# An SSM layer with a butterfly FFN on one core: another order of the work of its first two phases, and its step values brought to tokens by transposes

## What is computed

```
xn       = layernorm(x)
xi, z    = split(xn @ in_proj.T)               # 512 and 512 features
xc       = silu(conv of 4 taps over time(xi) + conv_b)
d, B, C  = xc @ x_proj.T                       # 1 + 16 + 16 values per token
delta    = softplus(d)
h        = h * exp(-delta * exp(A_log)) + xc * delta * B     # the scan, state of 512 x 16
y        = (h @ C + xc * D) * silu(z)
x        = x + y @ out_proj.T
h        = butterfly_up(layernorm(x) @ W_exp + b_exp)        # 1024 features, 10 stages of 2 x 2 mixings
x        = x + butterfly_down(gelu(h + up_bias)) @ W_con + b_con + down_bias
```

## Time and profile before

| | us |
| --- | --- |
| median of 3 runs | 568.64 (566.94 to 570.74) |
| the profiled execution | 569.59, its span 567.9 |
| TensorE busy | 528.9 (93% of the span), weight loads 430.3 (76%) |
| VectorE busy | 409.6 (72%) |
| ScalarE busy | 306.1 (54%) |
| GpSimd busy | 109.5 (19%) |
| mean granted clock of TensorE | 0.966 |

### The profile page before, as it was taken

How to read it: one execution, slowest core, us unless ns; L and a number is a source line. 1 busy time by engine, 2 the same in 40 slices (tenths; PEclk the granted TensorE clock), 3 DMA queues, 4 the chain that set the end, 5 groups by cost and what they waited for, 6 DMA issues and landing times.

```text
span 567.9 us, 8152 instructions
## 1 busy us (share of the span) xinstructions
PE 528.9 (93%) x2996; PEld 430.3 (76%) x2996; DVE 409.6 (72%) x860; ACT 306.1 (54%) x526; POOL 109.5 (19%) x96
## 2 busy tenths in 40 slices
PE   3998899888999999999999999999999999699896
PEld 3766676776897779887888778877888788578886
DVE  4859999587983799468966799379946894575532
ACT  2876883865239622874268623962287417431342
POOL 4042100230201301050103120130105021411110
PEclk9986979799999999999999999999999999799999
DMA  8542311200012001210112001200021002100011
GB/s 244 97 27 3 80 35 38 76 2 2 23 52 74 4 2 48 66 39 2 37 41 74 0 9 68 71 8 1 5 73 38 0 2 74 41 1 0 6 34 37
DMA packets 42619, 21.75 MB, mean 38 GB/s; under 512 B 26419, under 2 KB 41011, under 8 KB 42580
## 3 DMA queue, kind: packets, MB, share of 16 engines
q1 hardware_dynamic: 39940, 17.57, 13.0%
q10 hardware_dynamic: 2640, 3.67, 2.3%
HBM read 16.78 MB, written 4.46 MB: 37 GB/s over the span
## 4 chain that ended last, share of the span: by engine, by line
PE 48%; DVE 20%; issue 12%; ACT 9%; SPq 6%; POOL 3%; DMA 0%; DVEq 0%; ACTq 0%; POOLq 0%
PE wide L711 12%; PE acc L844 9%; PE wide L833 7%; SPq L420 5%; PE wide L822 4%; DVE xc L1552 2%; DVE xc L1555 2%; POOL x1b_xn L598 2%; DVE state L1516 2%; DVE hid_low L1429 2%; PE wide L804 2%; PE small L731 2%; PE wide L811 2%; DVE xc L1412 2%; ACT L1054 2%
## 5 line engine op out<-in xcount | busy, mean ns | idle before, releaser
L1054 ACT ACTIVATE hid_f<-wide,bias_up 128x512 f32<-128x512 f32 x64 | 44.0, 687 | 162.0 <-PE wide L833 161.6
L1412 DVE SCALAR_TENSOR_TENSOR xc<-xi,taps,xc 128x512 f32<-128x512 f32 x96 | 87.0, 911 | 4.0 <-ACT xc L1085 1.7
L844 PE MATMUL acc<-w_down_high,hid_high 128*128 128x256 f32 x256 | 73.2, 286 | 5.6 <-DVE hid_low L1429 5.4
L844 PE MATMUL acc<-w_down_high,hid_low 128*128 128x256 f32 x256 | 71.9, 281 | 0.0
L844 PE MATMUL acc<-w_down_low,hid_high 128*128 128x256 f32 x256 | 71.9, 281 | 0.0
L1429 DVE TENSOR_TENSOR hid_low<-hid_f,hid_high 128x512 fp32r<-128x512 f32 x64 | 46.3, 725 | 29.8 <-ACT hid_high L1163 29.2
L833 PE MATMUL wide<-xnT_ln2T_high,w_up_high 128*128 128x512 f32 x128 | 55.4, 432 | 3.4 <-DVE xnT_ln2T_low L1423 1.8
L522 POOL TENSOR_TENSOR rstd<-var_eps,minus_half 128x4 f32<-128x4 f32 x16 | 19.1, 1192 | 202.8 <-DVE var_eps L1317 202.8
L711 PE MATMUL wide<-xnT_ln1T_high,w_in_high 128*128 128x512 f32 x128 | 56.5, 441 | 1.1 <-DVE xnT_ln1T_low L1423 1.0
L822 PE MATMUL wide<-w_out,xc 128*128 128x256 f32 x256 | 56.7, 379 | 0.3 <-DVE xc L1555 0.3
L844 PEld LDWEIGHTS acc<-w_down_high,hid_high 128*128 128x128 f32 x256 | 48.0, 188 | 11.2 <-issue 8.2
(11 more groups left out here) (185 smaller groups left out, 1054.6 us busy)
## 6 DMA issues: line engine op xcount, KB each, us to landing
x_res<-in_L_attn_x_dram SPq DMA_DIRECT2D x9, 512.0 KB, 3.5
c_near<-c_of_tokens SPq DMA_DIRECT2D x8, 512.0 KB
out_dram<-x1b_xn SPq DMA_DIRECT2D x8, 512.0 KB, 2.9
x_ln<-in_L_attn_x_dram SPq DMA_DIRECT2D x7, 512.0 KB, 3.6
xc<-in_L_attn_in_proj_w_dram ACTq DMA_DIRECT2D x2, 512.0 KB, 7.1
xc<-in_L_ffn_W_exp_dram ACTq DMA_DIRECT2D x1, 1024.0 KB, 10.8
x1b_xn<-in_L_ffn_W_con_dram ACTq DMA_DIRECT2D x1, 1024.0 KB, 14.5
raw_out<-n_L_attn_out_proj_w_dram ACTq DMA_DIRECT2D x1, 512.0 KB, 7.0
```

What stands on the lines that cost most here:

```text
L844: last = pe.matmul(acc[:, c, :], hid[h][:, j % HRING, c * P:(c + 1) * P], w_down[w][:, j, 0:DM], start=j == 0 and c % 2 == 0 and n == 0, s ...
L1054: ins = act.activation(out_ap, in_ap, how.pop("func"), **how)
L1412: ins = dve.scalar_tensor_tensor(xc[u % BATCH][:, e, :], xi[:, e, tap:tap + TILE], taps[:, e, tap:tap + 1], xc[u % BATCH][:, e, :], ALU.mu ...
```

## The change

Three things are changed, in phases 0 and 1 but for the first.

- `xd_tokens_first` transposes the blocks of `xdT` against the identity, 128 x 128 each, in place of multiplying them by `fold`; VectorE adds the two halves as it takes them, with a `tensor_reduce` in place of the copy. `fold` and its semaphore go.
- In phase 0, B comes ahead of the second unit's first input projection; the C products and the state inputs follow after four projections, and the steps of the weights are placed anew. On VectorE the convolutions are spread over the phase, and the diagonal comes behind them; `advance_state` comes ahead of `assemble`, and the third DOWN mixing, the short and whole DOWN paths and the third unit's normalisation come behind the gates. On ScalarE the first DOWN scaling comes behind the first two taps, the silu of z 0 and of x 1 ahead of later copies, and only the first UP scaling is left in phase 0. VectorE waits for the zeroed tiles later.
- In phase 1, VectorE does all three UP mixings, ScalarE the second and third scalings, the weights' steps come later, and w_down is made in two steps (17 and 18).

```diff
         w_x = sb("w_x", [P, CB, HALF])
-        fold = sb("fold", [P, XD])
         w_out = sb("w_out", [P, CB, DM])
...
         rates_exp = sem("rates_exp")
-        folded = sem("folded")
         made = sem("made")
...
 [("w_up", 1, 0), ("w_up", 1, 1)],
-[("w_down", q, 0) for q in range(4)],
+[("w_down", q, 0) for q in range(2)],
+[("w_down", q, 0) for q in range(2, 4)],
         ]
...
     for c in range(GR):
-        last = pe.matmul(bank[:, c * P:c * P + XD], xdT[:, c * P:(c + 1) * P], fold[:, :], start=True, stop=True)
+        last = pe.transpose(bank[:, c * P:(c + 1) * P], xdT[:, c * P:(c + 1) * P], ident[:, :])
     mark_written(last, "xdtok", 0, u)
...
     tokens_first(0)
-    pe.wait_ge(folded, 1)
     xd_tokens_first(0)
+    transposes(1, "ln1T", x_ln, norm1)
     prepare(4)
     prepare(5)
-    prepare(6)
-    transposes(1, "ln1T", x_ln, norm1)
     pe.wait_ge(masks_made, 2)
...
     step_sums(0)
+    decayed_b(0)
     in_projection(1, 0)
-    prepare(7)
     in_projection(1, 1)
-    decayed_b(0)
-    prepare(8)
+    prepare(6)
     in_projection(1, 2)
-    decayed_c_start(0)
-    prepare(9)
+    prepare(7)
     in_projection(1, 3)
+    decayed_c_start(0)
     decayed_c_block(0)
-    prepare(10)
-    in_projection(1, 4)
     state_inputs(0)
-    prepare(11)
+    prepare(8)
+    in_projection(1, 4)
+    prepare(9)
     in_projection(1, 5)
-    prepare(12)
-    in_projection(1, 6)
     off_diagonal(0)
+    prepare(10)
+    in_projection(1, 6)
+    prepare(11)
     in_projection(1, 7)
+    prepare(12)
     prepare(13)
     ssm_output(0)
-    prepare(14)
-    transposes(2, "ln1T", x_ln, norm1)
     wait_all_taken("w_out")
     out_projection(0, 0)
+    transposes(2, "ln1T", x_ln, norm1)
+    prepare(14)
     out_projection(0, 1)
...
     in_or_none(v, 5)
-    beside("in 5")
     decayed_c_start(u)
     in_or_none(v, 6)
-    beside("in 6")
     decayed_c_block(u)
     state_inputs(u)
+    beside("state inputs")
     in_or_none(v, 7)
+    beside("in 7")
     off_diagonal(u)
...
     up(p, 2)
+    beside("up 2")
     down(p, 0)
...
 def weights_of_ffn(place):
-    if place == "in 5":
+    if place == "state inputs":
         prepare(15)
-    elif place == "in 6":
+    elif place == "in 7":
         prepare(16)
     elif place == "products":
+        prepare(17)
         wait_all_taken("w_up")
     elif place == "up 1":
-        prepare(17)
+        prepare(18)
+    elif place == "up 2":
         wait_all_taken("w_down")
...
     exp_abs(0)
+    high_parts(1, "ln1T")
     prepare(4)
     prepare(5)
-    scale_blocks(DOWN, 0)
     place_halo(1)
-    high_parts(1, "ln1T")
     exp_sums(0)
-    scale_blocks(DOWN, 1)
+    exp_gaps(0)
     first_tap(1, 0)
-    scale_blocks(DOWN, 2)
     first_tap(1, 1)
-    exp_gaps(0)
-    prepare(8)
-    first_tap(1, 2)
-    take_c_start(0)
+    scale_blocks(DOWN, 0)
     exp_diagonal(0)
-    prepare(9)
+    first_tap(1, 2)
     first_tap(1, 3)
     save_halo(1)
+    take_c_start(0)
     take_c_block(0)
-    prepare(10)
-    copy_z(1, 4)
     copy_first_state(0)
-    prepare(11)
+    scale_blocks(DOWN, 1)
+    prepare(8)
+    copy_z(1, 4)
+    prepare(9)
     copy_z(1, 5)
-    prepare(12)
-    copy_z(1, 6)
-    copy_z(1, 7)
     silu_z(0)
+    prepare(10)
+    copy_z(1, 6)
+    prepare(11)
     silu_x(1)
+    copy_z(1, 7)
+    prepare(12)
+    scale_blocks(DOWN, 2)
     silu_z(1)
     scale_blocks(UP, 0)
-    scale_blocks(UP, 1)
     high_parts(2, "ln1T")
...
     exp_sums(u)
+    beside("sums")
     if v < UNITS:
...
         copy_z(v, 5)
+    beside("gaps")
     take_c_start(u)
     exp_diagonal(u)
-    beside("diagonal")
     if v < UNITS:
...
         copy_z(v, 7)
+    beside("z 7")
     copy_first_state(u)
+    beside("first state")
     gelu(p, 0)
...
 def weights_of_ffn(place):
-    if place == "abs":
+    if place == "sums":
+        scale_blocks(UP, 1)
+    elif place == "gaps":
         scale_blocks(UP, 2)
-    elif place == "diagonal":
-        prepare(15)
     elif place == "z 6":
+        prepare(15)
+    elif place == "z 7":
         prepare(16)
-    elif place == "gelu 1":
+    elif place == "first state":
         prepare(17)
+    elif place == "gelu 1":
+        prepare(18)

...
     dve.wait_ge(rates_exp, 1)
-    dve.tensor_tensor(fold[:, :], ident[:, 0:XD], ident[:, HALF:HALF + XD], ALU.add).then_inc(folded, 1)
     dve.tensor_reduce(row_in_block[:, :], ident[:, :].rearrange("p (j u) -> p u j", u=BL), AXIS_X, ALU.add)
...
                            rates[:, :].unsqueeze(1).to_broadcast([P, NB, NS]), ALU.mult))
-    dve.wait_ge(zeroed, 2)

...
     written(dve, u, "xdtok", 0)
-    mark_read(dve.tensor_copy(xd[:, :, :], tile_of("xdtok", 0, u)[:, :]
-                              .rearrange("p (c w) -> p c w", w=P)[:, :, 0:XD]), "xdtok", 0, u)
+    mark_read(dve.tensor_reduce(xd[:, :, :], tile_of("xdtok", 0, u)[:, :]
+                                .rearrange("p (c h w) -> p c w h", h=2, w=HALF)[:, :, 0:XD, :], AXIS_X, ALU.add), "xdtok", 0, u)
     read(dve, u, "xdtok", 0)
...
     take_xd(0)
+    dve.wait_ge(zeroed, 2)
     softplus(0)
-    multiply_short_paths(UP)
-    sum_biases()
     low_parts(1, "ln1T")
     take_sums(0)
-    add_blocks(DOWN, 0)
-    add_blocks(DOWN, 1)
-    multiply_whole_paths(UP)
+    sum_biases()
     weigh(0)
-    add_blocks(DOWN, 2)
     weigh_b(0)
-    for e in range(CB):
-        convolve(1, e)
+    convolve(1, 0)
+    multiply_short_paths(UP)
+    add_blocks(DOWN, 0)
+    convolve(1, 1)
+    multiply_whole_paths(UP)
+    convolve(1, 2)
+    convolve(1, 3)
+    add_blocks(DOWN, 1)
     diagonal_times_c(0)
     sum_diagonal(0)
-    assemble(0)
     advance_state(0)
-    multiply_short_paths(DOWN)
+    assemble(0)
     first_stats(2)
...
     gate(0, 1)
-    first_normalise(2)
     gate(0, 2)
     gate(0, 3)
+    first_normalise(2)
+    multiply_short_paths(DOWN)
+    add_blocks(DOWN, 2)
     multiply_whole_paths(DOWN)
-    add_blocks(UP, 0)
-    add_blocks(UP, 1)
+    low_parts(2, "ln1T")
     first_residual(0, 0)
...
     second_stats(0)
-    low_parts(2, "ln1T")
     second_normalise(0)
...
     softplus(u)
-    low_parts(p, "ln2T")
     beside("softplus")
+    low_parts(p, "ln2T")
     take_sums(u)
     weigh(u)
+    beside("sums")
     weigh_b(u)
...
     if place == "softplus":
-        add_blocks(UP, 2)
+        add_blocks(UP, 0)
+    elif place == "sums":
+        add_blocks(UP, 1)
     elif place == "weighed":
+        add_blocks(UP, 2)
         low_of_ffn(("w_up", 0, 0), ("w_up", 0, 1), ("w_up", 1, 0), ("w_up", 1, 1))
+        low_of_ffn(*(("w_down", q, 0) for q in range(2)))
     elif place == "assembled":
-        low_of_ffn(*(("w_down", q, 0) for q in range(4)))
+        low_of_ffn(*(("w_down", q, 0) for q in range(2, 4)))

```

More of the change, by code:

```diff
@@ L1255, in weights_of_ffn @@
             def weights_of_ffn(place):
-                if place == "abs":
+                if place == "sums":
+                    scale_blocks(UP, 1)
+                elif place == "gaps":
                     scale_blocks(UP, 2)
-                elif place == "diagonal":
+                elif place == "z 6":
                     prepare(15)
-                elif place == "z 6":
+                elif place == "z 7":
                     prepare(16)
+                elif place == "first state":
+                    prepare(17)
                 elif place == "gelu 1":
-                    prepare(17)
+                    prepare(18)
             prepare(0)
@@ L1636, in phase @@
                 softplus(u)
+                beside("softplus")
                 low_parts(p, "ln2T")
-                beside("softplus")
                 take_sums(u)
                 weigh(u)
+                beside("sums")
                 weigh_b(u)
```

42 lines of the change are left out of this document (21 added, 21 removed).

## The result

The changed kernel takes 572.25 us (median of 20 runs, 568.82 to 574.91); the kernel before took 568.62 us beside it (20 runs). One run of the kernel before took 746.18 us, and the ratio is of the others. The ratio is 1.0068, with a 95% interval from 1.0055 to 1.0082: 0.7% slower, where 567.0 was forecast. Its profiled execution took 572.39 us (span 570.7), that of before 569.59.

A forecast was written before the change was run, and what follows sets the result against it. TensorE was taken to bound from 137.29 us on, before it VectorE's written order with TensorE's clock. Terms +0.3 - 2.4 = -2.1 us from 569.59 gave 567.5, or 566.5 against the median; 567.0 was said, range 559 to 574.5.

The forecast's parts named there:

- Part 1: Transposes in place of the fold's matmuls: 0.47 us off in each of phases 2 to 6, about 2.4 us.
- 0.47: Saving in us for each of phases 2 to 6: fold holds the chain 0.91 us, four transposes 0.44.
- Phase 7 gives nothing: No saving in phase 7: TensorE waits for softplus, which waited 0.88 us for ScalarE's exp, not for xd.
- Rival 3: Transposes lower the clock in the steady phases, costing 3.4 to 10 us: 574.5 us; chance 0.06.
- Part 2: New orders of phases 0 and 1, laid out step by step from 32 us on: +0.3 us.
- the walk: Paper timeline of phases 0 and 1 with the trace's durations: first down product at 139.0 against 138.75, +0.3 us.
- 1.45, 1.35, 1.75, 2.3 and 3.2: Phase 1 TensorE stops: FFN input's low part, gap's exponential, B hat, w_up transposes, low parts of w_down and hidden block.
- Loss 0.9: End of phase 0: gates no longer hidden by transposes and prepare 14; out projection ends at 97.8, not 96.9.
- TensorE, now at full clock, waits twice more ... reaches its transposes of w_up: Phase 1: waits of 1.35 and 1.75 us, w_up transposes reached at 121.5, then a 2.3 us stop.
- rival 2: Clock falls in new places in phases 0 and 1: +4.8 to +6.5 us, 574 to 576 us; chance 0.15.
- as now: Behind the first down product nothing is late but TensorE, as in the kernel before.
- Rival 1: Half of phase 1's 10 us of stops vanish, and 1 us before prepare 8: 561.5 or 560.5 us; chance 0.25.

The follow-up runs named there:

- e1: Only the transposes and the pairwise sum, on the kernel before with its order of work kept: 566.48 us, ratio 0.996.
- e10: Changed kernel plus 16 unread 128x512 products in TensorE's waits of phase 1: 570.74 us, ratio 1.0041.
- e12: Kernel before with transposes, second unit's transposes and high and low parts early, B ahead of the first projection: 564.60 us, ratio 0.9919.
- e13: Changed kernel with pre-gate idle filled, first UP mixing in phase 0, gates hidden, plus whole UP paths ahead of the second convolution: 568.67 us.
- e3: Changed kernel with third DOWN mixing and short DOWN paths ahead of the gates, first UP mixing back in phase 0: 569.21 us, ratio 1.0015.
- e6: Changed kernel with the low part of the FFN's input ahead of the first UP mixing in phase 1: 572.20 us, ratio 1.0073.
- e16: e11 with phase 0's end as before (gates covered), third unit's low part still ahead of the UP mixings: 566.88 us, ratio 0.9988.
- e15: e12 with third unit's transposes and prepare 14 behind the first half of out projection, normalising behind all gates: 571.39 us, ratio 1.0062.
- e11: Kernel before with transposes and the whole new order of phase 0, phase 1 as before, two UP mixings ending phase 0: 572.71 us, ratio 1.0065.
- e14: e12's phase 0 without its two UP mixings, plus the changed phase 1, which does all three: 572.51 us, ratio 1.0065.
- e4: Changed kernel with prepare 14 and third unit's transposes ahead of out projection, short paths before the gates, normalising between gates: 568.61 us, ratio 1.002.
- e8: e1 with the third unit's high and low parts ahead of the second scaling and both UP mixings: 568.24 us, ratio 1.0001.

## Why the prediction was wrong

**Part 1 was right in kind and size, with two terms off.** It gave 2.4 us; e1 measured 2.3 (0.4%). The term "0.47" a phase came out as 0.37 to 0.42. "Phase 7 gives nothing" came out as 1.5 us in these two profiles, but e10, e12 and e13, with transposes, have 86.7 to 86.8 us there as the fold has, and the others 84.6 to 85.5: how long the clock stays low in phase 7 differs, and two profiles with the fold don't tell whether the transposes shorten it. The sum over pairs took 0.43 us (0.5 said). Rival 3 didn't come: the clock is 1.00 from 165 to 232 us with sixteen and four transposes in a row. The rule of the Trainium skill, "TensorE: Matmul & The Clock Gate", Part 4: PE-mode transpose, is neither shown nor refuted by it, but the price that it would have had was not paid.

**Part 2: the stops came where the walk put them.** Read against it (the changed kernel started 1.04 us late): B's transposes ended at 41.20, said 42.4, since the clock had not fallen yet in this execution. The timeline of TensorE of the changed kernel:

```profile
41.20 0.48 PE L710 MATMUL wide<-xnT_ln1T_high,w_in_high 128*128 128x512 f32 x1
...
49.23 3.78 PE L651 MATMUL acc<-low_w,hid_f 2*128 2x512 f32 x4
...
69.74 1.14 PE L664 MATMUL acc<-mixed,x_res 128*128 128x257 f32 x4 [1.02 <-ACT mixed L1029]
...
74.19 2.80 PE L651 MATMUL acc<-low_w,hid_f 8*128 8x256 f32 x12 [1.05 <-ACT mixed L1029]
...
88.05 5.38 PE L821 MATMUL wide<-w_out,xc 128*128 128x256 f32 x16 [2.18 <-DVE xc L1560]
...
96.14 3.72 PE L821 MATMUL wide<-w_out,xc 128*128 128x256 f32 x16
99.79 1.94 PE L720 MATMUL wide<-xc,w_x 128*64 128x512 f32 x8
...
114.50 1.16 PE L759 MATMUL small<-after,gap_w 128*128 128x128 f32 x8 [1.28 <-DVE xnT_ln2T_low L1428]
...
120.10 0.66 PE L769 MATMUL small<-ident,cbd_tok 128*128 128x128 f32 x4 [0.78 <-ACT b_hat L1055]
...
122.83 1.91 PE L780 MATMUL small<-x_tok,b_end 128*16 128x512 f32 x8 [2.07 <-DVE b_hat L1507]
...
126.10 1.94 PE L668 MATMUL acc<-ident,mixed 128*128 128x128 f32 x8 [1.36 <-DVE mixed L1397]
...
143.41 0.55 PE L843 MATMUL acc<-w_down_high,hid_high 128*128 128x256 f32 x1 [3.46 <-DVE hid_low L1434]
```

Before prepare 8 no wait shows, since the clock fell to half at 47.6 and TensorE filled the time by being slow; e3, where it didn't, has 3.78, and e6, whose order of phase 0 is that of the changed kernel, 3.8 (3.6 said). The two waits for ScalarE's banks are 1.02 and 1.05 (1.1 and 1.6 said). In phase 1 the walk had 1.45, 1.35, 1.75, 2.3 and 3.2, together 10.05; measured are 1.28, 0.78, 2.07, 1.36 and 3.46, together 8.95.

**What failed is what the walk took at full clock.** Less the late start, it is behind by 0.95 us where the out projection ends (99.79 against 97.8), by 1.06 where softplus ends (109.0 against 106.9) and by 1.3 at the transposes of w_up (126.10 against 123.8). At the first down product it is behind by 3.4 (143.41 against 139.0). Three steps of the prediction failed.

First, "Loss 0.9" at the end of phase 0: it was 1.9. The out projection started 0.8 us earlier than the walk had it (88.05 against 87.8, less the late start), but behind a stop of 2.18 us and at half clock: its first half took 5.38 us, its second 3.72.

Second, "TensorE, now at full clock, waits twice more ... reaches its transposes of w_up", with "the w_up and w_down hand-overs" behind it: 17.3 us from there to the first down product, where the walk had 15.2. The kernel with the filler, whose clock stays high there, takes 16.2 (125.83 to 142.03). So two things were left out, about 1 us each:
- The clock. It fell behind the stops of 0.78 and 2.07 us, and the state inputs and the first transposes of w_up took 1.91 and 1.94 us, in e10 1.05 and 1.06. That was a mechanism of rival 2, which asked "about 2 us in a row".
- VectorE's stop beside GpSimd. The sum of the UP bias is 0.17 us before and 2.21 here, ahead of the low part of w_up. First VectorE's timeline of the changed kernel, then GpSimd's:

```profile
122.70 3.26 DVE L1397 SCALAR_TENSOR_TENSOR mixed<-mixed,high_w 128x257 f32<-128x257 f32 x8
125.99 2.21 DVE L1402 TENSOR_TENSOR bias_up<-mixed,up_bias_sb 128x8 f32<-128x8 f32 x1
128.12 1.28 DVE L1338 TENSOR_TENSOR w_up_low<-acc,w_up_high 128x512 fp32r<-128x512 f32 x2
```

```profile
125.24 2.93 POOL L590 TENSOR_TENSOR diag<-diag,dB 128x1024 f32<-128x1024 f32 x1 [6.12 <-ACT diag L1145]
```

Not all of it shows: ScalarE has the high part ready at 127.8, so 0.3 us. With the clock high, in e10, the high part is ready at about 127.0 and the low part still starts at 127.87; there the stop costs 0.8. The two hide each other in part. ScalarE's and VectorE's timelines of e10:

```profile
126.49 1.09 ACT L1026 ACTIVATE w_up_high<-acc 128x512 fp32r<-128x512 f32 x2 [1.13 <-PE acc L668]
```

```profile
127.87 1.27 DVE L1348 TENSOR_TENSOR w_up_low<-acc,w_up_high 128x512 fp32r<-128x512 f32 x2
```

Third, behind the down product the walk had TensorE "as now"; it took 1.46 us more to the next mark (37.22 us, 35.76 before), with a second fall of 3.4 us at 143 us, behind the stop of 3.46. All nine kernels with this stop show such a fall at their first down product (between 136 and 148 us).

In the profiled execution the terms are then: late start +1.04, walk +3.37, behind it +1.46, phases 2 to 6 +0.5 (1.84 saved of 2.35), phase 7 -1.48: +4.9 over the 567.5 forecast for it, which is 572.4.

**Rivals.** Rival 2 came in part, and by its own sign (the first down product at 142 or later, with a clock of 0.5 between 115 and 135). Its falls at the gates and before prepare 15 are there; its clock at half through the second projection, with VectorE's chain 1.9 us later, is not, as the clock fell only at 47.6 us. Measured are 572.25 us where it said 574 to 576; it stood at 0.15, the forecast at 0.50. Rival 1, which wanted half of the 10 us of stops in phase 1 to vanish, got 1.1 us of them. The weighing failed at one point. The walk carried its gains at full clock (no 2.09 us wait, no fall at 102.7) and its stops without the falls that the trace shows behind such stops. The kernel before has 27.2 us of half clock from 28 to 160 us; the walk had about 14 (37.5 to 45.0, and the 6.8 us from 75 us on that it left); the changed kernel has 27.2 again.

**Where the 8 us of the order lie.** Shown: the early start and B first gain (e12, 0.4% on e1). The rest of the new middle, with the third unit's low part ahead of the UP mixings, takes back 0.7% (e12 to e16). The bare gates cost 1.4% by themselves on e12 (e15), and 0.8% on the new middle (e16 to e11, where the short paths and the third DOWN mixing go behind the gates too). The new phase 1 costs 1.5% by itself on e12 (e14). On the bare gates it costs nothing more (e11 to the changed kernel), and with the gates hidden, on the new middle, 0.3% (e16 to e4, which also differ in the place of the third DOWN mixing). So these losses overlap, and no one size belongs to each. One reason shows in the waits: in e15 the late low part of the third unit stops TensorE for 5.2 us, with two UP mixings and the residual ahead of it. In the changed kernel the low part stands ahead of the residual and the mixings are in phase 1, so this wait is gone (1.00 at 97 to 105 us), but the mixings stop TensorE there. VectorE's work is the same everywhere; by this reading, what the order decides is whether it fits into idle time. The change leaves VectorE idle for 5.59 us ahead of the first gate, and has 6.4 us of UP mixing more in phase 1. VectorE's timeline of the changed kernel:

```profile
81.33 0.75 DVE L1557 SCALAR_TENSOR_TENSOR xc<-xc,skip,wide 128x512 f32<-128x512 f32 x1 [5.59 <-PE wide L810]
```

Removing a single stop gave nothing in e6 and e13 because other stops grew by as much: the sums of their waits did not fall. Open: why e8 lost 0.4%; and how much of the 8 us, and of the loss in e14 and e15, is the clock, as each has falls of its own.

## What to carry to other kernels

When a hand-written order is laid out on paper, give each long stop of TensorE the clock's fall that the traces show behind stops of its length, or else the new order is compared with a trace that has paid for its own. Here a fall stood behind the stops of 3.46, 2.18 and 2.07 us, and none behind those of 1.51 and 1.61 us of the kernel before. Judge a moved step by the idle time of the busy engine that it leaves behind and fills: two edits that fill the same idle time are worth little more than one, and a stop that is removed gains only if the sum of the stops falls. And try the parts of a change apart: here the transposes, the early second unit and B first gain 0.8%, and two other parts of the same change lose more than that each when put on top of it.

## What the runs showed of the hardware

- VectorE's sum of 128x8 elements from two SBUF tiles took 2.21 us beside a GpSimd product of 2.93, and 0.17 alone. The Trainium skill, "SBUF — State Buffer", Who interferes with whom, says that a VectorE instruction with two inputs in SBUF contends with a GpSimd instruction that reads SBUF, and that the order of issue decides which of the two stops. The trace agrees: the sum began 0.75 us behind GpSimd's start and ended as that did (128.20 and 128.17 us).
- Four fp32 transposes of 128x128 hold the chain for 0.44 to 0.49 us, eight records of the fold's matmul, 128x33 out of the same operands, for 0.91.
- Executions of the same kernel differ by 3.4 us with their mean granted clock (0.963 and 0.975): a single profile can't settle 2 us.
